# Moving the normalisation of x2 from VectorE to ScalarE, one step of the order later

## What is computed

```python
x = x + tanh(g_xattn[0]) * xattn(layernorm(x), ctx, ctx)   # 32 query heads, 8 key/value heads, D = 16
x = x + tanh(g_ffn[0])   * ffn(layernorm(x))               # shared expert, and 4 of 32 routed experts
# layernorm(x) = (x - mean) / sqrt(var + 1e-5), over the 512 features of a token
```

## Time and profile before

| | us |
|---|---|
| runs of the kernel before | 2306.51, 2306.56, 2308.84 |
| their median | 2306.56 |
| the profiled execution's own time | 2309.02 |
| its span in the trace | 2307.2 |

### The profile page before, as it was taken

The page is one execution under the profiler, slowest core; times in us unless marked ns, Lnnn a source line. Parts: engine busy times, 40 slices in busy tenths (PEclk is TensorE's granted clock), DMA queues, the critical chain, the costliest instruction groups (busy, mean ns, idle before and its releaser), DMA issues.

```text
span 2307.2 us, 43358 instructions
## 1 busy us (share of the span) xinstructions
PE 2250.8 (98%) x13953; PEld 1735.8 (75%) x13953; DVE 1150.2 (50%) x2218; ACT 763.7 (33%) x1312; POOL 593.1 (26%) x1395
## 2 busy tenths in 40 slices
PE   6999999999997999999999999999999999999999
PEld 5777777777776877777777777778777777777777
DVE  6999999999997723222232222223222232223232
ACT  5888888888883101010110101101010110101010
POOL 5677777777763100000000000000000000000100
PEclk9999999999998999999999999999999999999999
DMA  3555555555553133222223221222222223222321
GB/s 83 147 146 144 146 146 150 144 144 146 143 159 127 10 120 118 85 84 80 65 94 107 84 80 64 80 81 101 84 84 80 68 93 105 84 80 92 121 67 43
DMA packets 269455, 235.14 MB, mean 102 GB/s; under 512 B 120545, under 2 KB 196321, under 8 KB 269410
## 3 DMA queue, kind: packets, MB, share of 16 engines
q1 hardware_dynamic: 265058, 221.89, 32.0%
q0 software_dynamic: 4352, 12.65, 1.9%
HBM read 161.88 MB, written 71.57 MB: 101 GB/s over the span
## 4 chain that ended last, share of the span: by engine, by line
PE 68%; DVE 1%; DMA 0%; issue 0%; DVEq 0%; POOLq 0%
PE acc L1128 7%; PE p_u L1144 7%; PE p_u L1145 7%; PE p_u L1146 7%; PE acc L1130 7%; PE acc L1129 7%; PE p_g L1144 7%; PE p_g L1146 7%; PE p_g L1145 7%; PE p_x L1176 2%; PE p_y L1163 2%; PE p_x L1163 2%; PE p_x L1154 0%; DMA rows<-out_dram 0%; PE p_y L1169 0%; DVE rows L1108 0%
## 5 line engine op out<-in xcount | busy, mean ns | idle before, releaser
L1062 DVE TENSOR_TENSOR act_f<-p_u,act_f 128x512 f32<-128x512 f32 x176 | 121.7, 692 | 984.9 <-PE p_u L1146 984.8
L967 ACT ACTIVATE act_f<-p_g 128x512 f32<-128x512 f32 x176 | 105.3, 598 | 1215.8 <-PE p_g L1146 1194.8
L561 DVE TENSOR_REDUCE negmax<-p_max 128x8 f32<-128x1024 f32 x256 | 312.6, 1221 | 43.6 <-PE p_max L713 43.6
L1128 PE MATMUL acc<-wd_h,hh 128*128 128x512 f32 x704 | 279.5, 397 | 0.0
L1144 PE MATMUL p_u<-xh,wgu_h 128*128 128x512 f32 x704 | 274.8, 390 | 3.6 <-DVE act_f L1062 3.6
L1144 PE MATMUL p_g<-xh,wgu_h 128*128 128x512 f32 x704 | 275.7, 392 | 0.0
L1145 PE MATMUL p_u<-xl,wgu_h 128*128 128x512 f32 x704 | 274.6, 390 | 0.0
L1146 PE MATMUL p_u<-xh,wgu_l 128*128 128x512 f32 x704 | 274.4, 390 | 0.0
L1129 PE MATMUL acc<-wd_l,hh 128*128 128x512 f32 x704 | 274.3, 390 | 0.0
L1130 PE MATMUL acc<-wd_h,hl 128*128 128x512 f32 x704 | 274.2, 390 | 0.0
L1146 PE MATMUL p_g<-xh,wgu_l 128*128 128x512 f32 x704 | 274.2, 390 | 0.0
(11 more groups left out here) (142 smaller groups left out, 3465.5 us busy)
## 6 DMA issues: line engine op xcount, KB each, us to landing
ew<-in_L_ffn_Wg_dram SPq DMA_DIRECT2D x32, 704.0 KB
ew<-in_L_ffn_Wu_dram SPq DMA_DIRECT2D x32, 704.0 KB
xs<-in_x_dram SPq DMA_DIRECT2D x64, 256.0 KB, 2.7
xres<-in_x_dram SPq DMA_DIRECT2D x64, 256.0 KB, 2.8
out_dram<-x SPq DMA_DIRECT2D x64, 256.0 KB, 2.7
xn_rows<-xn SPq DMA_DIRECT2D x64, 256.0 KB, 3.0
xn_cols<-xnT SPq DMA_DIRECT2D x64, 256.0 KB, 3.3
rows<-out_dram SPq DMA_DIRECT2D x16, 1024.0 KB, 5.2
```

What stands on the lines that cost most here:

```text
L561: nc.vector.tensor_reduce(negmax[c // 2][:, :].rearrange("p (g c i) -> p c i g", g=2, c=2)[:, c % 2, :, :], p_max[:, :, :].rearrange("p a ...
L1062: nc.vector.tensor_tensor(act_f[:, :], p_u[:, :], act_f[:, :], ALU.mult).then_inc(h_done, 1)
L1128: mm(acc[:, j, :], a[:, t], wd_h[:, f, :], start=(f == 0), stop=False)
```

## The change

VectorE's layer_norm of x2 in c = 3 is taken out. ScalarE computes the same as x2 * rs2 + nm2 with one activation (Identity, with a scale and a bias per row), where nm2 = -mean * rs2 is one more GpSimd instruction on 128 x 1. It stands in the next step, at the end of c = 0 behind qt, for batch B-3. The write of xn's rows on SyncE's queue moves from c = 0 to behind c = 3 of the same step. The write of x2 on VectorE gets a wait for the normalisation of the batch two before it, since that now reads x2 on another engine. GpSimd's function for rs2 is written out anew with the third instruction.

```diff
-            ve2, rs2 = sb("ve2", [128, 1]), sb("rs2", [128, 1])
+            ve2, rs2, nm2 = sb("ve2", [128, 1]), sb("rs2", [128, 1]), sb("nm2", [128, 1])
...
@@ SyncE
-                            if (B - 3).ok:
-                                b = B - 3
-                                wait(sp, xn_done, b.n + 1)
-                                sp.dma_start(xn_dram[bass.ts(b.n, 128), 0:E], xn[b.par][:, :]).then_inc(xn_out[b.par], 16)
                         if c == 1:
...
                             sp.dma_start(out_rows[bass.ts(b.n, 128), :], x2[b.par][:, :]).then_inc(x2_out[b.par], 16)
+                    if (B - 3).ok:
+                        b = B - 3
+                        wait(sp, xn_done, b.n + 1)
+                        sp.dma_start(xn_dram[bass.ts(b.n, 128), 0:E], xn[b.par][:, :]).then_inc(xn_out[b.par], 16)
                     if weights_load(B):
...
@@ GpSimd
+                def inverse_root_and_shift(b):
+
+                    pool.wait_ge(stat2, b.n + 1)
+                    alone(pool, spare_p)
+                    chain.inc(nc.gpsimd.tensor_scalar(ve2[:, :], mv2[b.par][:, 1:2], EPS, None, ALU.add))
+                    chain.wait(pool)
+                    wait(pool, xn_done, b.n)
+                    alone(pool, spare_p)
+                    chain.inc(nc.gpsimd.tensor_tensor(rs2[:, :], ve2[:, :], mhalf[:, :], ALU.pow))
+                    chain.wait(pool)
+                    alone(pool, spare_p)
+                    nc.gpsimd.tensor_scalar(nm2[:, :], mv2[b.par][:, 0:1], rs2[:, 0:1], -1.0, ALU.mult, ALU.mult).then_inc(rs2_done, 1)
...
                     if (B - 2).ok:
-                        inverse_root(B - 2, stat2, mv2, ve2, rs2, xn_done, rs2_done)
+                        inverse_root_and_shift(B - 2)
...
@@ ScalarE
+                def norm_x2(b):
+                    act.wait_ge(rs2_done, b.n + 1)
+                    wait(act, xnT_mm, b.n - 1)
+                    wait(act, xn_out[b.par], 16 * b.half)
+                    nc.scalar.activation(xn[b.par][:, :], x2[b.par][:, :], ACT.Identity, bias=nm2[:, 0:1], scale=rs2[:, 0:1]).then_inc(xn_done, 1)
...
                         if c < 3 and B.ok:
                             q_evac(B, c + 1)
+                        if c == 0 and (B - 3).ok:
+                            norm_x2(B - 3)
                         if c == 3 and (B + 1).ok:
...
@@ VectorE
                             wait(dve, x2_out[b.par], 16 * b.half)
+                            wait(dve, xn_done, b.n - 1)
                             nc.vector.scalar_tensor_tensor(x2[b.par][:, :], o_sb[:, :], tanh_x[:, 0:1], xres[b.par][:, :],
                                                            ALU.mult, ALU.add).then_inc(x2_done, 1)
...
-                        if c == 3 and (B - 2).ok:
-                            b = B - 2
-                            wait(dve, xnT_mm, b.n - 1)
-                            wait(dve, xn_out[b.par], 16 * b.half)
-                            layer_norm(b, x2, mv2, rs2, rs2_done, xn, xn_done)
```

More of the change, by code:

```diff
@@ L400, in body @@
                         nc.gpsimd.tensor_tensor(w_cols(wgu_l, B.pair), wst_cols, w_cols(wgu_h, B.pair).bitcast(F32), ALU.subtract).then_inc(wlo_done, 1)
-                chain.per_turn = 2 * (1 + 1 + 1 + 1 + 1)
+                chain.per_turn = 2 * (1 + 2 + 1 + 1 + 1)
                 iterations(pool, body, chain)
```

## The result

The changed kernel took 2347.59 us (median of 4 runs, 2347.09 to 2349.40), beside 2307.70 for the kernel before on the same chip: ratio 1.0174, 95% interval 1.0157 to 1.0192, 40 us slower. Its profiled execution took 2349.40 us, with a span of 2347.6. The forecast was 2341.6, within 2325 to 2359.

A forecast was written before the change was run, and what follows sets the result against it. A ring of handovers in the first phase was taken to bound, not one engine. 61 steps x 0.54 = 32.9 us plus 2.1 at the end give +35.0, 2341.6 us against the median of 2306.56; range 2325 to 2359.

The forecast's parts named there:

- What bounds: First phase: a ring of handovers, not one engine; period 10.62 us, read from VectorE's reductions of chunk 0.
- VectorE's part: Normalisation taken off VectorE: of 0.77 us per batch at most 0.25 comes back at once, 16 us in all.
- rival 1: Transpose of xn in c = 1: its wait vanishes, VectorE's relief gains 16 us, 2290.6; chance 0.07.
- GpSimd's part: Third GpSimd instruction, nm2: adds 0.45 us, with 1.0 us of cover before ScalarE wants it; costs nothing.
- SyncE's part: Write of xn's rows, 0.37 us of the queue, moves from c = 0 behind c = 3; costs nothing.
- ScalarE's part and the ring: ScalarE's exponential of c = 3 through qt, activation (0.74) and TensorE back: 11.16 us against 10.62, 0.54 per step.
- The signs to look for: Trace after: period 11.1 to 11.2 us, xn wait 0.8 to 1.0, VectorE busy 49 less, p_max wait 70 or more.
- 2: First phase: TensorE takes up more of the delay, period stays 10.62, 2306.6 us within 0.2%; chance 0.05.
- 3: ScalarE's activation takes 0.88 us, 2350.6, or nm2 comes 0.2 us beyond its cover, 12 us; chance 0.17.
- 4: Two table loads of 1.283 us per batch on ScalarE, 164 us more, 2506; chance 0.03.

The follow-up runs named there:

- relief run: Kernel before, with VectorE normalising only 8 of 512 columns and ScalarE getting nothing: 2300.02 us, ratio 0.9963.
- nm2 alone: Kernel before with only GpSimd's third instruction (nm2) added: 2315.36 us, ratio 1.0033.
- plain copy: Changed kernel with a copy of x2 in place of the activation's scale and bias per row: 2336.17 us, ratio 1.0119.
- doubled: Changed kernel with a second activation of the same shape and operands ahead of the new one, into an unread tile: 2395.17 us, ratio 1.0372.
- the run without nm2: Kernel before with only the moved write of xn's rows and the extra wait ahead of x2: 2308.84 us, ratio 1.0003.
- older xn: Changed kernel with TensorE transposing the xn of one batch earlier: 2301.37 us, ratio 0.9972.
- both places: Changed kernel with the activation ahead of qt and the transposes of xn behind p_ot of c = 1: 2301.72 us, ratio 0.9976.

## Why the prediction was right

**What bounds.** Right: a ring of handovers, and not a full engine. After the change TensorE is at 91% and VectorE at 89%, and the kernel is slower. The prediction did not name the ring that makes the 10.62 before. The rows show it: p_mt in c = 2 (413.96), TensorE without a marked wait to p_max of chunk 3, VectorE without one from its reduction (417.50) to that of chunk 1 (423.17), and p_mt again, which waits 0.30 us for it (424.44). The normalisation lies in it.

**VectorE's part.** This part failed. "The reductions start 0.36 and 0.15 us later" than p_max ends was read as wait for VectorE; 0.15 of each is the handover, which the relief run shows with VectorE idle. The relief is worth 8 us, not 16. The forecast did not use it, since another ring closed last, but rival 1 was promised twice the gain that was there: it should have had 2299, not 2290.6.

**GpSimd's part.** The third instruction took 0.267 us, and 0.21 of handover ahead of it:

```profile
406.43 0.27 POOL L344 TENSOR_SCALAR nm<-mv,rs 128x1 f32<-128x1 f32 x1 [0.21 <-POOL rs L341]
```

0.48 together for my 0.45. nm2 is there at 406.70 and ScalarE wants it at 408.62, 1.9 us of cover. "Nothing" is right for the wait. What I did not think of is that a shifted GpSimd instruction can lengthen one of VectorE's, which cost the kernel before 7.7 us. The longer x2 of the changed kernel (0.95 us at 412.82, 1.24 at 423.89) is another matter: with nm2 alone x2 took 810 ns, less than the 850 before. It overlaps GpSimd's second qs instruction, and that became shorter as x2 became longer (L362 948 ns before, L375 740 after), so the two changed sides as their starts moved. It costs nothing here: in three kernels in which this ring closes x2 took 896, 1059 and 799 ns (plain copy, changed, doubled), and the step followed the activation alone.

**SyncE's part.** Right: nothing, as the run without nm2 shows.

**ScalarE's part and the ring.** Right in its places and in all terms but one: 0.74 us for the activation should have been 0.80. This 0.06 and 0.03 in the handovers make 61 x 0.09 = 5.5 us; the end of the phase takes back 0.4. That is the difference of 4.9 between the 39.9 us measured and the 35.0 forecast, within rounding. The plain copy and the doubled activation show that the length goes into the step in full.

**The signs to look for.** The period (11.1 to 11.2) came out as 11.25, just above; the wait for xn (0.8 to 1.0) as 0.82 and 1.13, 0.98 on average; p_mt behind the logits by 0.41; the second phase unchanged. Two were wrong. VectorE's busy time was to fall by 49 us and fell by 6 on the page (1150.2 to 1144.2), as x2 and is_top took 23 us more and the others overlap less (the durations of all its instructions fell by 22.8 us in sum). Its wait for p_max was to grow to 70 us or more between 200 and 700 us and grew from 21.1 to 36.6: VectorE's idle time did double (10.0 to 21.2 of 200 us), but part of it went to slower instructions and to other waits, rec for p_ot among them.

**The rivals.** 1 and 2 did not come; 3 did not either: the activation stayed below 0.88, and between 200 and 700 us it never waited for nm2. 4 did not: no table load was added, and the activation stands back to back with copies and exponentials.

**What stays open.** Three different kernels end at a step of 10.50 (relief alone, older xn, both places). Which ring closes there was not tested. In the relief run p_mt in c = 2 still waits for the reduction of chunk 1 in both steps (0.35 us, and 0.30 in this row):

```profile
420.20 0.28 PE L705 MATMUL p_mt<-ident,negmax 128*16 128x128 f32 x1 [0.30 <-DVE negmax L563]
```

So there it is the ring of before, now closed by TensorE's p_max of chunk 0 instead of VectorE's c = 3. With both places moved p_mt waits in one step of two only (0.19 us). A GpSimd order that keeps its long instructions off VectorE's was not tried with both places moved.

## What to carry to other kernels

Moving work to the engine with the most idle time helps only if it lands where that engine is idle and before its consumer asks: here 0.80 us on an 86% busy engine cost 0.63 us per step at one place of the order, and nothing once the consumer stood behind two groups that did not need the result. Sum the ring through the new producer and its consumer from rows of the kernel before, start to start and with the waits left out, and compare it with the period; then shorten it by moving the producer ahead of, or the consumer behind, what need not be in it. Earlier is not always better: the place must also lie behind its own inputs, and what is queued behind it must not be what another engine waits for.

## What was not expected of the hardware

- A VectorE instruction of 128 x 512 with operands per row took 0.54 us alone, 0.99 or 1.30 us beside a GpSimd subtraction of 0.95, and ended 0.28 us after it in both cases. A new 0.27 us instruction on GpSimd, which moved that subtraction, cost the kernel before 7.7 us.
- Identity with scale and bias per row took 797 ns on ScalarE for 512 columns, a plain copy 612.
- From p_max of chunk 0 to its reduction pass 0.15 us even when VectorE is idle; at chunk 3, the rows show 0.04 (p_max from 412.50 for 0.72, reduction at 413.26 in the relief run). The ends of matmuls are modelled in the profile, so part of the difference may lie in them.
